# One core, eight stages: expert layers begun inside the attention before them, one function set for the small heads' activations, transposed values in full attention

## The reference

```python
x = x + linear_attention(_layernorm(x))    # 8 heads of 128, chunks of 64
x = x + windowed_blocks(_layernorm(x))     # two layers: windowed attention (8 heads of 64), gated FFN
x = x + small_head_attention(_layernorm(x))  # 16 query heads of 8: global, then a window of 32
x = x + windowed_blocks(_layernorm(x))
x = x + head_attention(_layernorm(x))      # per token: 16 heads attend to each other
x = x + experts(_layernorm(x))
x = x + full_attention(_layernorm(x))      # 2 heads of 64, 512 x 512 scores per batch
x = x + experts(_layernorm(x))
```

```python
logits = xf @ Ws.T + bs
probs = softmax(logits); routes = argmax(probs); pmax = max(probs)
xf = xf * pmax[:, None]
perm = argsort(routes, stable=True)
y = relu(xs @ W1[e] + b1[e]) @ W2[e] + b2[e]     # xs = xf[perm]
out = y[rs, arange]                              # so row i of the sum gets the i-th row of the sorted order
```

## Time and profile before

| | us |
|---|---|
| median of 3 runs (lowest, highest) | 1912.55 (1907.21, 1919.57) |
| the profiled execution | 1910.82 |
| its span | 1909.0 |
| small heads | 719 to 1030 |
| head attention | 1435 to 1582 |
| experts 0, with the rows' return | 1582 to 1684 |
| full attention | 1684 to 1809 |
| experts 1 | 1809 to 1909 |

### The profile page before, as it was taken

One profiled execution on the slowest core, in us unless ns is written; L12 is line 12 of the kernel. 1 busy time (PEld: TensorE's weight loads), 2 busy tenths in 40 slices (PEclk: granted clock), 3 DMA queues, 4 the chain that ended last, 5 costly groups with the idle time before them and its releaser, 6 DMA issues. The chain is left out here.

```text
span 1909.0 us, 37673 instructions
## 1 busy us (share of the span) xinstructions
PE 1589.8 (83%) x13078; PEld 1134.5 (59%) x13078; DVE 1245.5 (65%) x3810; ACT 1073.6 (56%) x2763; POOL 973.7 (51%) x732
## 2 busy tenths in 40 slices
PE   5999997889999777899787889999866757949787
PEld 5999995556666543344454566666644545637555
DVE  3555553998888744555763898888736975646465
ACT  3656653778888734566542688888832113324332
POOL 1333333888878612223443888878714673431044
PEclk9999998999999986899776899999987886979789
DMA  5000000111111100000000111111100001210012
GB/s 210 1 1 1 1 1 4 30 33 27 32 27 26 28 5 1 1 1 1 1 1 1 26 33 32 28 28 31 27 6 1 1 0 39 23 28 1 21 25 23
DMA packets 41082, 38.63 MB, mean 20 GB/s; under 512 B 21944, under 2 KB 32192, under 8 KB 40512
## 3 DMA queue, kind: packets, MB, share of 16 engines
q1 hardware_dynamic: 35264, 32.02, 6.5%
q0 software_dynamic: 5632, 4.20, 1.8%
HBM read 13.14 MB, written 4.20 MB: 9 GB/s over the span
## 5 line engine op out<-in xcount | busy, mean ns | idle before, releaser
L970 ACT ACTIVATE arena<-ps 128x512 f32<-128x512 f32 (+5 forms) x680 | 367.5, 571 | 329.2 <-PE ps L326 99.4
L1209 ACT ACTIVATE arena<-ps 128x320 f32<-128x320 f32 (+4 forms) x256 | 132.5, 561 | 136.5 <-PE ps L677 133.7
L1126 ACT ACTIVATE arena<-arena,g_small 128x128 f32<-128x128 f32 x512 | 197.8, 391 | 0.5
L2184 POOL TENSOR_TENSOR arena<-arena,consts 128x512 f32<-128x512 f32 (+1 forms) x64 | 93.2, 1456 | 195.3 <-ACT arena L1209 195.2
L1677 DVE CUSTOM_DVE_ANT_0 arena<-ps,consts,g_ss 128x128 f32<-128x128 f32 x512 | 146.7, 341 | 43.2 <-PE ps L520 43.2
L677 PE MATMUL ps<-arena 32*128 32x160 f32 (+4 forms) x1024 | 123.0, 471 | 23.0 <-ACT arena L1209 10.5
L326 PE MATMUL ps<-consts,arena 128*128 128x128 f32 x400 | 79.8, 335 | 64.8 <-DVE arena L1465 13.7
L2234 POOL TENSOR_TENSOR g_ss<-g_ss,consts 128x8 f32<-128x8 f32 x64 | 108.3, 1692 | 44.2 <-DVE g_ss L1707 40.5
L677 PEld LDWEIGHTS ps<-arena 32*128 32x128 f32 x1024 | 62.1, 214 | 91.3 <-ACT arena L1209 54.4
L326 PEld LDWEIGHTS ps<-consts,arena 128*128 128x128 f32 x400 | 54.3, 169 | 96.2 <-DVE arena L1465 17.5
L1549 DVE TENSOR_REDUCE arena<-arena 128x8 f32<-128x1032 f32 x32 | 39.3, 1228 | 110.7 <-ACT arena L1027 110.7
(11 more groups left out here) (257 smaller groups left out, 4230.5 us busy)
## 6 DMA issues: line engine op xcount, KB each, us to landing
arena<-arena SPq DMA_DIRECT2D x112, 128.0 KB, 2.3
weights<-in_w SPq DMA_DIRECT2D x1, 5069.0 KB, 24.2
weights<-in_w SPq DMA_DIRECT2D x1, 2052.0 KB, 12.7
arena<-Y SPq DMA_DIRECT2D x64, 32.0 KB
arena<-Y SPq DMA_DIRECT2D x64, 31.8 KB
consts<-in_c SPq DMA_DIRECT2D x1, 1278.0 KB, 8.9
sorted_rows<-X SPq DMA_DIRECT2D x1, 1024.0 KB, 5.1
X<-sorted_rows SPq DMA_DIRECT2D x4, 256.0 KB, 3.6
```

What stands on the lines that cost most here:

```text
L970: copy = lambda o, i: act.activation(o, i, ACT.Copy)
L1126: last = act.activation(g_p[:, n % 2, 4 * hf + i, :], g_sc[:, 4 * hf + i, :], ACT.Exp, scale=-1.0, bias=g_mn[:, h:h + 1], accum_out=g_rs[: ...
L1209: act.activation(b_p[:, U % 2, 2 * gp:2 * gp + 2, at:at + n], ps[:, b:b + 2, 0:n], ACT.Exp, scale=float(HD) ** -0.5).then_inc(s.b_exp, 1)
L2184: pool.tensor_tensor(v, v, m.unsqueeze(1).broadcast_to([P, NG, n]), ALU.mult)\
```

## The change

1. The drains and the meeting points between head attention and experts 0, and between full attention and experts 1, are gone. Front 0 of the experts is issued at chosen steps of the attention stage; the units follow the attention's last steps on each engine; fronts 1 to 3 begin at units 0, 7 and 14 (`turned_at`), and the indices are made after unit 19. In head attention the last tile's `values`, and the last batch's turn, projection and addition, move among units 3 to 7. The experts have their own space in the arena, other PSUM banks (transposes, logits and ranks share one), and their own statistics. The first unit writes e_acc by a multiplication; the biases of batch 0 are gathered beside it and added by POOL later.
2. Before its first unit, small-head attention loads on ACT one function set that holds both Exp and Ln.
3. In full attention `values` has 64 columns of values as the stationary side and the transposed probabilities moving, so its result comes out transposed, head 0 in partitions 0 to 63 and head 1 in 64 to 127 of one bank. It runs one step later. The turn of the output (L833) and its normalisation before it (L1927) are gone; two projections, one per head, follow (`rows_out(n, 0)`, `rows_out(n, 1)`), and DVE adds each to X, scaled by the head's reciprocal sum.

The new `variance`, `centre`, `shift_routed`, `route`, `prefix` and `places_of_all` are the old nested functions with other operands' places.

```diff
-        m_os, m_oT = carve(P), carve(P)
-        m_rs = sb("m_rs", [P, 2, 2])
+        m_oT = carve(P)
+        m_rs = sb("m_rs", [P, 4, 2])
         m_rn = sb("m_rn", [P, 16])
 
-        taken[0] = 0
...
+        front_bank, up_banks, down_banks = (4, 7), ((0, 1), (5, 6)), ((2, 3), (0, 1))
+        turned_at = (None, 0, 7, 14)
...
-                for t in range(-3, TT + 3):
+                for t in range(-3, TT):
...
+                        turn_sums((t - 6) // NT)
                         rows_out((t - 6) // NT)
+                    if t == 10:
+                        turn_routed_x(0, 0)
+                    if t == 11:
+                        logits(0, 0)
+                    if t == 13:
+                        turn_scaled_x(0, 0)
+                    if t == 14:
+                        ranks(0, 0)
+                experts(0, turn_sums, rows_out)
 
...
                     need(pe, s.m_out, n)
-                    for h in range(2):
-                        for j in range(NT):
-                            last = mm(ps[:, 4, h * DF:(h + 1) * DF], m_pT[:, n % 2, h, j, :],
-                                      m_v[:, z % 2, j, h * DF:(h + 1) * DF], start=j == 0, stop=j == NT - 1)
+                    for j in range(NT):
+                        for h in range(2):
+                            last = mm(ps[h * DF:(h + 1) * DF, 4, 0:P], m_v[:, z % 2, j, h * DF:(h + 1) * DF],
+                                      m_pT[:, n % 2, h, j, :], start=j == 0, stop=j == NT - 1, skip_group_check=True)
                     last.then_inc(s.m_pv, 1)
 
-                def turn_out(n):
-                    pe.wait_ge(s.m_os, n + 1)
+                def rows_out(n, h):
+                    rows = slice(DF * h, DF * h + DF)
+                    pe.wait_ge(s.m_oT, n + 1)
                     need(pe, s.m_out, n)
-                    tr(ps[:, 4, P:2 * P], m_os, ident).then_inc(s.m_oT_ps, 1)
-
-                def rows_out(n):
-                    pe.wait_ge(s.m_oT, n + 1)
-                    mm(ps[:, 4, 2 * P:3 * P], m_oT, W("d_wo"), start=True, stop=True).then_inc(s.m_rows, 1)
-
-                for t in range(-5, TT + 2):
+                    if h:
+                        pe.wait_ge(s.m_row0, n + 1)
+                    mm(ps[:, 4, P * (h + 1):P * (h + 2)], m_oT[rows, :], W("d_wo")[rows, :], start=True, stop=True)\
+                        .then_inc(s.m_row1 if h else s.m_row0, 1)
+
+                for t in range(-5, TT + 3):
                     if rows_at(t):
                         scores(t)
-                    if rows_at(t - 2):
...
+                    if rows_at(t - 2):
+                        values(t - 2)
+                    if t == 9:
+                        turn_routed_x(1, 0)
+                    if t == 12:
+                        logits(1, 0)
+                    if t == 14:
+                        turn_scaled_x(1, 0)
+                    if t == 15:
+                        ranks(1, 0)
+                experts(1)
...
+                    if k == 0 and q == 6:
+                        turn_sums(NB - 1)
+                    if k == 0 and q == 7:
+                        rows_out(NB - 1)
+                    for c in range(1, NB):
+                        if q == turned_at[c]:
+                            turn_routed_x(k, c)
+                        elif q == turned_at[c] + 1:
+                            logits(k, c)
+                        elif q == turned_at[c] + 5:
+                            turn_scaled_x(k, c)
+                        elif q == turned_at[c] + 6:
+                            ranks(k, c)
 
...
+                act.add_instruction(mybir.InstLoadActFuncSet(name=nc.get_next_instruction_name(), act_func_set_id=6))
...
+                    if t in (9, 13):
+                        norm_routed(0, t // NT - 2)
+                    if t == 10:
+                        keep_routed_x(0, 0)
+                    if t == 12:
+                        exps_routed(0, 0)
+                    if t == 13:
+                        keep_scaled_x(0, 0)
+                exps(TT - 1)
+                experts(0, keep_sums)
...
+                    if t in (8, 12, 16):
+                        norm_routed(1, t // NT - 2)
+                    if t == 9:
+                        keep_routed_x(1, 0)
+                    if t == 13:
+                        exps_routed(1, 0)
+                    if t == 14:
+                        keep_scaled_x(1, 0)
...
+                    if t == 12:
+                        shift_routed(0, 0)
...
+                    if t == 13:
+                        route(0, 0)
+                    if t == 15:
+                        prefix(0, 0)
...
+                    if t in (7, 11, 15):
+                        add_rows((t - 7) // NT)
+                    if t in (8, 12):
+                        variance(0, t // NT - 2)
+                    if t in (9, 13):
+                        centre(0, t // NT - 2)
+                shift(TT - 1)
+                values(TT - 2)
+                sums(TT - 1)
+                variance(0, 2)
+                experts(0, values, add_rows)
...
+                def add_rows(n):
+                    x, r = X[:, n, :], m_rs[:, n % 4, :]
                     dve.wait_ge(s.m_ri, n + 1)
-                    need(dve, s.m_oT_ps, n)
-                    heads = lambda a: a.rearrange("p (h d) -> p h d", h=2)
-                    tt(heads(m_os), heads(ps[:, 4, 0:P]), wide(m_rs[:, n % 2, :], [P, 2, DF], 2), ALU.mult)\
-                        .then_inc(s.m_os, 1)
-
-                def add_rows(n):
-                    x = X[:, n, :]
-                    dve.wait_ge(s.m_rows, n + 1)
                     dve.wait_ge(s.m_xb, n // NT + 1)
-                    tt(x, x, ps[:, 4, 2 * P:3 * P], ALU.add).then_inc(s.m_out, 1)
-
-                for t in range(-9, TT + 2):
+                    dve.wait_ge(s.m_row1, n + 1)
+                    stt(x, ps[:, 4, P:2 * P], r[:, 0:1], x, ALU.mult, ALU.add).then_inc(s.m_half, 1)
+                    dve.wait_ge(s.m_half, n + 1)
+                    stt(x, ps[:, 4, 2 * P:3 * P], r[:, 1:2], x, ALU.mult, ALU.add).then_inc(s.m_out, 1)
+
+                for t in range(-9, TT + 3):
...
+                    if t == 13:
+                        shift_routed(1, 0)
+                    if t in (6, 10, 14):
+                        dve.wait_ge(s.m_out, t - 2)
+                        variance(1, t // NT - 1)
+                    if t in (7, 11, 15):
+                        centre(1, t // NT - 1)
+                    if t == 14:
+                        route(1, 0)
...
+                variance(1, 3)
+                prefix(1, 0)
+                experts(1)
...
-                    else:
+                    elif q:
                         dve.wait_ge(es.e_acc_in, (n - 1) * k + q)
                     for j in range(NT):
                         i = NT * c + j
-                        ins = stt(e_acc[:, i, :], ps[:, 6 + q % 2, j * P:(j + 1) * P], e_oh[:, i, e:e + 1],
+                        if q == 0:
+                            ins = ts(e_acc[:, i, :], ps[:, down_banks[k][0], j * P:(j + 1) * P], e_oh[:, i, 0:1], None,
+                                     ALU.mult)
+                            continue
...
+                    if k == 0 and q == 3:
+                        values(TT - 1)
+                        centre(0, 2)
+                    if k == 0 and q == 7:
+                        add_rows(NB - 1)
+                        variance(0, 3)
+                    if q == (9 if k == 0 else 1):
+                        centre(k, 3)
+                    for c in range(1, NB):
+                        if q == turned_at[c]:
+                            shift_routed(k, c)
+                        elif q == turned_at[c] + 1:
+                            route(k, c)
+                        elif q == turned_at[c] + 5:
+                            prefix(k, c)
+                    if q == turned_at[3] + 5:
+                        places_of_all(k)
...
+                fetch_biases(0)
+                fetch_biases(1)
+                if k == 0:
+                    root_routed(0, 3)
+                fetch_biases(2)
+                pool.wait_ge(b2_sem[0], 16 * NT * (k + 1))
+                pool.wait_ge(es.e_acc_in, (E * NB - 1) * k + E)
+                pool.tensor_tensor(e_acc[:, 0:NT, :], e_acc[:, 0:NT, :], e_bias, ALU.add).then_inc(es.e_bias_in, 1)
+                fetch_biases(3)
                 pool.wait_ge(es.e_idx_in, k + 1)
                 pool.wait_ge(es.e_kept, 16 * (k + 1))
+                pool.wait_ge(es.e_bias_in, k + 1)
...
-            if STAGES >= 6:
+            if STAGES >= 7:
                 pool.wait_ge(batch_go, 6)
                 pool.sem_inc(batch_seen, 1)
-                asked.n = 0
-                experts(0)
-            if STAGES >= 7:
-                pool.wait_ge(batch_go, 7)
-                pool.sem_inc(batch_seen, 1)
                 full_attention()
-                pool.drain().then_inc(batch_done, 1)
```

(15 more changed lines are left out.)

439 lines of the change are left out of this document (195 added, 244 removed).

## The result

The changed kernel took 1888.47 us (median of four runs, 1885.27 to 1895.89) against 1916.06 for the kernel before, measured beside it: a ratio of 0.987, interval 0.985 to 0.990. The ratio makes it 25 us less (the two medians lie 27.6 apart). The forecast was 1857, 55 us less than before's own execution, with a range that ended at 1885. The direction was right, the size was under half, and the time lies outside the range.

The account below looks back on a forecast made before the run. No engine was taken to bound the whole span; at seams engines wait and PE's clock is low. Savings of 8.5 + 15 + 31.5 = 55 us took 1910.8 to 1855.8, median 1857; forecast case 1842 to 1870, range 1833 to 1885.

Parts of the forecast that it names:

- part 4: Seam before experts 1: last scores to last addition some 10 us instead of 17.3; units end 33.6 earlier, 31.5 after sends.
- Part 3: Full attention: shorter values save 0.7 us a step, 10 over 15 steps; 5 remain after routing work and PE's wait.
- Part 2: Seam after head attention: first unit 22.0 us earlier, less 3 of PE work, 2 of coupling, 2 for sends: 15 us.
- Part 1: Small heads: one function set replaces 14 table loads of 18.0 us in all; 8.5 us of it on the path.
- The clock's rival: Full attention: the clock drops and all steps run at 6.3 us instead of 4.7, +24 us, 1881; chance 0.12.
- More holds: Head attention: three more small DVE operations wait for POOL's mix, 16 us, later indices push sends 5: about 1877; chance 0.18.
- The slower case: Experts: units run at the lower clock, about 1.9 us more each; with all 64, +122 us, 1979; chance 0.05.
- The change of the array's form: Full attention: 32 changes between full array, row halves and column halves cost 0.21 us each, 7 us: 1864; chance 0.06.

Follow-up runs that it names:

- e2: Kernel before with only full attention's transposed values, one step later, and the two additions in place of one: ratio 0.9969.
- e9: Changed kernel with three products that nobody reads filling TensorE's wait at step 14 of full attention: ratio 0.9862.
- e13: Changed kernel with the same three products at step 14 as e9, measured again beside the changed kernel itself: ratio 0.9844.
- e4: Changed kernel with full attention's transposed values in bank 5 instead of 4 from row tile 10 on: ratio 0.9851.
- e8: Changed kernel with values in bank 5 from tile 10, fronts six units apart, second transposes and ranks a step later, first prefix at step 17: ratio 0.9751.
- e10: Changed kernel with the small layer-norm operations of head attention moved from VectorE to GpSimd: ratio 0.9753.
- e1: Kernel before with only the function set of exponential and logarithm loaded ahead of small-head attention: ratio 0.9978.
- e6: Changed kernel with the second transposes and ranks of the experts' first batch one step later in full attention: ratio 0.9854.

## Why the prediction was right and wrong

**The size.** Of the 55 us forecast the two profiles have 15 and the ratio 25. Of the 40 us that the profiles lack, 17.7 are in part 4's stretch.

**Right:** the direction, and head attention's loop. It grew by 14.7 us to products(15), forecast 13.5, and where it was said: steps 8, 9, 12 and 13 grew by 2.9, 2.8, 2.9 and 4.3 (forecast 2.9, 2.9, 2.9 and 4.7); step 14 grew by 1.6, which had no term. Also values of 1.06 us (1.09), PE's wait at step 14, seven pairs of table loads gone, and unit 0 free of its bias gather. The first unit's time, 1586.98 for 1587.3, is luck: it came 3.1 us later behind products(0) than forecast, and the stages ahead happened to be 3.4 shorter in that profile.

**The step that failed is part 4**, "afterwards the turn, one copy, values, one copy, two projections: some 10 us". It counted one chain where the later step leaves three (tiles 13, 14 and 15), one behind the other, since each values waits for the additions of the tile before it, both being in bank 4. And it took them at full clock, though the earlier trace rows showed 0.65 in the same stretch before. Seen were 23.8 us to the last addition. The two faults can be told apart. With three chains but without the idle time at step 14 it is 16.7 us (e2, at a mean clock of 0.82), and with that idle time filled 17.0 (e9) and 17.3 (e13): some 7 us for the chains, and 7 for the clock behind the idle time. The clock's part is 10 us to the end of the kernel. Another bank for the values takes 8.5 us off the way to the first product (e4, profile), partly the same us. With all of it repaired (e8) the last addition still comes 18.7 us behind the last scores, and in no run under 15.3, so 10 was too few for this form in any case.

From the last addition to DVE's first unit another 7.3 us were seen and 3.4 forecast. The forecast had only the variance and the prefix; TensorE's products and the ReLU of unit 0 stand there too, at a clock of 0.50, and TensorE's transposes waited 2.0 us for DVE's prefix. Together that is 31.1 us to the first unit in place of 13.4.

**Part 3's sizes.** The free step is 4.83 us, not 4.3: the ring that closes it is scores, maximum, additions, values, next scores, which the prediction did not see because it followed the wait that was removed and not the one that took its place. In e2's first three steps, which have no additions yet, a step takes 4.23 to 4.27. Still the steps alone gave 13 us (e2) where 10 were forecast. Too small was the term against them: 5 us for variances, shift, route and the wait at step 14, and 12 seen: 4.3 in step 14, 5.1 in the other steps with the front, and 2.5 of low clock in the first three. Of 5 us one came.

**Part 2's terms.** Between the first and the last unit 5 us more were forecast (3 of work, 2 of coupling) and 7.0 seen: batch 2's `centre`, behind values(15) on DVE, held ACT for 5.9 us and PE for 3.6. In e10, where GpSimd does it, ACT doesn't wait, and the units take 66.3 us in place of 71.0. The sends cost 4.6 and 4.4 us instead of 2 and 2: indices come with unit 20 of 32, 16 sends at a pitch of 1.86 us take 29.7 us, and the last unit ends 18.4 us behind the first send (1657.99 - 1639.55). The prediction had 21 to 24 us for these units.

**Part 1's size is not settled:** 8.5 forecast, 5.6 in the two profiles, 4 (-1 to 9) by e1.

**The last 2 us**, from the last send to the end, were in no term and no experiment was made for them: every profile of the changed kernel and its variants has 5.5, those of the kernel before, e1 and e2 3.3 to 3.4. What sets it stays open.

**The rivals.** The clock's rival named the low clock as a cost, but for the wrong place: it put the drop into all steps (they ran at 0.94), and the long drop came at step 14 and behind. More holds: the routing's product under a mix (2.54) was in the forecast's own terms, and no further one came in the loop. The slower case: the units of experts 1 were at 1.00 from 1816 on in the changed kernel. The change of the array's form: values were within 0.03 of the price without it.

## What to carry to other kernels

When a wait is removed, walk the same instruction's other waits one by one: the next in line was a buffer that the new form shares with a later stage. A software pipeline made deeper by a step pays for it where the loop ends; count those chains in full, at the clock that the rows show there. And look at what a small operation is held by or queued behind on its engine: moving operations of 128 x 4 elements to GpSimd gave 14.4 us in the loop, 9.9 of them in steps that the change hadn't touched, and 6.4 among the units' products.

## What the runs showed of the hardware

**VectorE held by GpSimd.** While GpSimd's mix runs (5.4 us, all operands in SBUF), VectorE's `tensor_scalar` and products or `scalar_tensor_tensor` with all operands in SBUF end with it: 0.9 to 3.6 us for 128 x 4 elements that take 0.15 to 0.17 alone. Reduces, reciprocals, the statistics' operations and operations with an operand in PSUM did not wait (0.13 to 0.25 for the first two). The Trainium skill (SBUF — State Buffer, Who interferes with whom) says that VectorE and GpSimd share a pair of ports under an exclusive lock, for VectorE in its two-port modes or with two SBUF inputs; by that rule, the trace agrees, down to which operations waited.

**One bank for two stages.** The wait before the values is the kernel's own semaphore: transposed values, row products and additions share bank 4 in different columns. The Trainium skill (PSUM — Partial Sum Buffer, PSUM bank collisions raise a hardware error) has it that two engines' accesses to one bank at once, a write and a read among them, are an error even at other addresses, if they are in the same quadrant of partitions; no run here shows the error, e4 only shows that another bank removes the wait, and what that is worth.

**Idle time and the clock.** An idle time of 3.2 us at step 14, among waits of 1.0, was followed by 0.50 for 23 us and 0.52 for 14 more. Filled with 2.2 us of products, the stretch began at 1.00. In e6 and e8 that wait was gone, and the half clock began behind the next idle time of 2.6 and 2.7 us. But a long idle time is neither needed for a low clock nor enough for a long one. The changed kernel had three us of half clock in step 13, behind waits of some 1.0 us, and with 4.3 us of idle time e4 had only some 6 us of it. No run here gives the rule.

**Columns of 64.** Values on two column halves took 1.09 us for 16 passes of 128 columns, against 1.97 for 16 passes of 64 columns on the full width, at the same clock; between them and the scores on row halves no gap shows.
